# Experts' products on fp32 operands in place of three products of split parts, in a gated attention and mixture-of-experts block

## The chip, the cores and the metric

The kernel runs on one NeuronCore of a Trainium2 chip. The metric is the device time of one execution in microseconds (us), as the median of three executions. TensorE multiplies; VectorE, ScalarE and GpSimd work beside it, and SyncE issues most DMAs.

## The reference, cut to what matters

The block takes 4096 tokens (32 sequences of 128) of width 256. First comes cross attention with 16 heads of 64, which ends in a residual sum. Then comes a mixture of 8 experts, to which the change belongs: every token is sent to its two best experts, each expert takes at most 1024 tokens, and the experts' outputs are weighted and added to the residual.

```
logits = xf @ gate_w.T;  scores = softmax(logits);  topv, topi = top_k(scores, 2)
gates = topv / sum(topv);  flat_idx = topi * cap + loc          # cap = 1024
disp[flat_idx] += xf * valid;  de = disp.reshape(8, 1024, 256)
h  = relu(einsum("ecd,ehd->ech", de, fc1_w) + fc1_b)            # 1024 hidden
eo = einsum("ech,ehd->ecd", h, fc2_w) + fc2_b
x  = x + tanh(g_ffn) * sum(gathered(eo) * gates)
```

All arrays are fp32.

## The kernel before, in words

The program has two parts in one block, each written out in full by Python loops, with one instruction stream per engine and semaphores between them.

`attention` handles 8 groups of 4 sequences. It projects queries, keys and values, forms scores, exponentials, transposes and weighted values, projects out, adds the residual, and routes the tokens. GpSimd then scatters each token's normalised row into the table `disp` in device memory with 8 indirect DMAs for a group (`dispatch`, line 395). The last group's tail is `finish`, and each engine has one.

`experts` handles 8 experts of 1024 token slots each, in two halves of 512: 16 groups, numbered n = 2e + half. For a group, TensorE does the following in this order (line 1136 on):

- the upward products: 8 blocks m of 128 hidden units, each contracting two parts k of 128 features over 512 tokens, into one of two PSUM banks `up`;
- 8 transposes of the next group's rows into `rT` (line 1133);
- the downward products: for 4 blocks i of 128 tokens, 8 parts k of the hidden units, 256 output columns, into `down[i]`. Blocks 0 and 1 run interleaved, then block 2, then block 3.

Most of the kernel's large products don't take fp32 operands. An fp32 tensor is written as a high part (a copy to the type fp32r, on ScalarE: `high`, `split_high`, `high_rows`) and a low part (the tensor minus its high part, also fp32r: `low` and `low_rows` on VectorE, `split_low` on GpSimd). A product is then three: high by high, high by low, low by high (lines 1149 to 1151 and 1163 to 1165). Six fp32 uses remain: transposes, scores (L533), weighted values (L521), the routing logits (L565 and L648), the two rank products (L571 and L572), and the 16 filler products on the identity at the start (L109), which keep TensorE occupied while loads run.

For each expert SyncE loads `fc1` and `fc2` (1 MB each) into `w1_raw` and `w2_raw`. ScalarE and GpSimd split them into one of two pairs of split buffers. For expert 0 the split is made inside the attention's `finish`: two ScalarE copies (lines 740 and 748) and two VectorE subtractions (lines 962 and 986), which signal `s_e0_lo`. The hidden activations go from PSUM to `hid` by ScalarE with bias and relu (line 1199), then VectorE makes `hid_h` and `hid_l` (lines 1250 and 1252). After the downward products VectorE adds the bias (line 1259), ScalarE scales by the gate (line 1207) and GpSimd adds the rows into the output with 4 indirect DMAs for a group (line 1095).

Between the two parts TensorE runs fillers: 40 products on `wk_h` at the end of attention and 6 on `w1_h` ahead of the first expert group (line 1173).

Of the kernel before, what the change touches and what calls it, by code (L numbers as in the profile page):

```python
# [5 lines left out]
P = 128  # L6
# [64 lines left out]
def gated_block(nc, x, ctxT, g_x, g_f, wq, wk, wv, wo, bo, gateT, fc1T, fc1b, fc2, fc2b, out):  # L71
# [6 lines left out]
    with ExitStack() as keep:  # L78
# [17 lines left out]
        s_e0_lo = sem("e0_lo")  # L96
        shared = (s_e0_lo, first, blank, running, tanh_g, ident, w1_raw, w2_raw, w1_split, w2_split)
# [19 lines left out]
def attention(nc, ctx, block, sem, x_v, out_v, disp, ctxT, g_x, g_f, wq, wk, wv, wo, bo, gateT, fc1T, fc2, shared):  # L117
# [7 lines left out]
    s_e0_lo, first, blank, running, tanh_g, ident, w1_raw, w2_raw, w1_split, w2_split = shared  # L125
# [48 lines left out]
    def ps(name):  # L174
# [14 lines left out]
        s_dve_self, s_pool_self, s_dve_gate, s_pool_gate, s_e0_in, s_c0_hi, s_e0_hi,  # L189
# [8 lines left out]
        "dve_self", "pool_self", "dve_gate", "pool_gate", "e0_in", "c0_hi", "e0_hi",  # L198
# [239 lines left out]
    def _(pe):  # L438
# [185 lines left out]
        def wait_warm(count):  # L624
            keep_warm(nc, key_bank, wk_h[:, 0:P], wk_h[:, 0:TOK], count)
# [33 lines left out]
    def _(act):  # L659
# [73 lines left out]
        def finish():  # L733
# [5 lines left out]
            act.wait_ge(s_e0_in, 32)  # L739
            high(wq_h[:, :, :], w1_raw[:, :, :]).then_inc(s_e0_hi, 1)  # L740
# [6 lines left out]
            act.wait_ge(s_o_ready, 2 * NG)  # L747
            high(wo_h[:, :, :], w2_raw[:, :, :]).then_inc(s_e0_hi, 1)
# [6 lines left out]
    def _(dve):  # L755
# [195 lines left out]
        def finish():  # L951
# [9 lines left out]
            dve.wait_ge(s_e0_hi, 1)  # L961
            low(wq_l[:, :, :], w1_raw[:, :, :], wq_h[:, :, :]).then_inc(s_e0_lo, 1)
# [31 lines left out]
def experts(nc, ctx, block, sem, out_rows, disp, fc1T, fc1b, fc2, fc2b, shared):  # L994

    f32, f32r, i32, u32 = mybir.dt.float32, mybir.dt.float32r, mybir.dt.int32, mybir.dt.uint32
    ALU, ACT, AX = mybir.AluOpType, mybir.ActivationFunctionType, mybir.AxisListType.X
# [5 lines left out]
    s_e0_lo, first, blank, running, tanh_g, ident, w1_raw, w2_raw, w1_split, w2_split = shared  # L1003
    w1_h, w1_l = [w1_split[0], sb("w1_h1", [P, DK, H], f32r)], [w1_split[1], sb("w1_l1", [P, DK, H], f32r)]
    w2_h, w2_l = [w2_split[0], sb("w2_h1", [P, HK, D], f32r)], [w2_split[1], sb("w2_l1", [P, HK, D], f32r)]
    eo = [sb(f"eo_{n}", [P, GB, D]) for n in range(2)]
    rT_h, rT_l = sb("rT_h", [P, DK, TOK], f32r), sb("rT_l", [P, DK, TOK], f32r)
    hid = [sb(f"hid{n}", [P, TOK]) for n in range(2)]
    sb("line_up_hid", [P, LINE_UP])
    hid_h, hid_l = sb("hid_h", [P, HK, TOK], f32r), sb("hid_l", [P, HK, TOK], f32r)  # L1010
# [8 lines left out]
    def ps(name):  # L1019
# [7 lines left out]
        s_w_in, s_w_hi, s_w_lo, s_b_in0, s_b_in1, s_rows0, s_rows1,  # L1027
        s_rt_ready, s_rt_hi, s_rt_split, s_up_ready, s_hid, s_hid_hi, s_hid_split, s_down_ready, s_eo_raw,
        s_eo_raw2, s_eo_ready, s_scatter0, s_scatter1, s_meta, s_dve_self, s_pool_gate,
    ) = (sem("e_" + name) for name in (  # L1030
        "w_in", "w_hi", "w_lo", "b_in0", "b_in1", "rows0", "rows1",
        "rt_ready", "rt_hi", "rt_split", "up_ready", "hid", "hid_hi", "hid_split", "down_ready", "eo_raw",
# [4 lines left out]
    biases = [s_b_in0, s_b_in1]  # L1037

    disp_v = disp.rearrange("(e s) w -> e s w", e=E)
    EB = 2  # L1040
    TURNS = E // EB

    @block.sync
    def _(sp):
# [4 lines left out]
        def step(e, nxt, par, first=False):  # L1049

            if first:
                sp.wait_ge(s_e0_lo, 2)
            else:
                sp.wait_ge(s_w_lo, e)
            load_expert(sp, fc1T, fc2, nxt, w1_raw, w2_raw, s_w_in)
            if not first:
                sp.wait_ge(s_eo_raw2, 2 * e)
            load_bias(nxt, 1 - par)
            for half in range(2):
                n = 2 * e + half  # L1060
                sp.wait_ge(s_meta, n + 1)
                load_rows(nxt, half)
# [8 lines left out]
        step(0, 1, 0, True)  # L1071
        step(1, 2, 1)
        for t in range(1, TURNS - 1):
            for i in range(EB):
                step(EB * t + i, EB * t + i + 1, i)
        step(E - 2, E - 1, 0)
        step(E - 1, E - 1, 1)
        sp.wait_ge(s_w_in, 32 * E)
        sp.wait_ge(biases[0], 32 * (E // 2 + 1))
        sp.wait_ge(biases[1], 32 * (E // 2))  # L1080
        for half in range(2):
            sp.wait_ge(rows_in[half], 16 * (E + 1))
            sp.wait_ge(scatters[half], 16 * GB * E)

    @block.gpsimd
    def _(pool):
        def scatter(n, e, par, half):
            if half == 0 and not (isinstance(e, int) and e == 0):
                for done in scatters:
                    pool.wait_ge(done, 16 * GB * e)  # L1090
# [10 lines left out]
        def split_low(e, par):  # L1101

            pool.wait_ge(s_w_hi, 2 * e - 1)
            for k in range(DK):
                nc.gpsimd.tensor_tensor(w1_l[par][:, k, :], w1_raw[:, k, :], w1_h[par][:, k, :].bitcast(f32), ALU.subtract)
            pool.wait_ge(s_w_hi, 2 * e)
            nc.gpsimd.tensor_tensor(w2_l[par][:, :, :], w2_raw[:, :, :], w2_h[par][:, :, :].bitcast(f32),
                                    ALU.subtract).then_inc(s_w_lo, 1)

        def step(e, par):  # L1110

            split_low(e + 1, 1 - par)
            for half in range(2):
                scatter(2 * e + half, e, par, half)

        step(0, 0)
        step(1, 1)
        for t in range(1, TURNS):
            for i in range(EB):
                step(EB * t + i, i)  # L1120
# [4 lines left out]
    def _(pe):  # L1125
        mm = nc.tensor.matmul

        def transpose_rows(loads, half):

            pe.wait_ge(rows_in[half], loads)  # L1130
# [5 lines left out]
        def group(n, e, par, half):  # L1136

            for m in range(HK):
                if not (isinstance(n, int) and n == 0 and m < 2):
                    pe.wait_ge(s_hid, 8 * n + m - 1)  # L1140
                if m == 0:
                    pe.wait_ge(s_rt_split, 2 * n + 2)
                    if isinstance(e, int) and e == 0:
                        pe.wait_ge(s_e0_lo, 2)
                    else:
                        pe.wait_ge(s_w_lo, e)
# [7 lines left out]
            transpose_rows(16 * (e + 1) if half == 0 else 16 * (e + 2), 1 - half)  # L1154

            for k, i in [(k, i) for tiles in ((0, 1), (2,), (3,)) for k in range(HK) for i in tiles]:
                if i == 0:
                    pe.wait_ge(s_hid_split, 8 * n + k + 1)
                if k == 0 and not (isinstance(n, int) and n == 0):
                    pe.wait_ge(s_eo_raw, 4 * n - 3 + i)  # L1160
                t = slice(i * P, (i + 1) * P)
                o = down[i][:, 0:D]
# [136 lines left out]
```

## Time and profile before

| | us |
|---|---|
| time, median of 3 runs | 1035.96 (1035.08 to 1039.14) |
| profiled execution, its own time | 1036.79 |
| profiled execution, its span | 1034.9 |
| TensorE busy | 962.2 (93%) |
| VectorE busy | 642.1 (62%) |
| ScalarE busy | 504.6 (49%) |
| GpSimd busy | 359.9 (35%) |
| TensorE's share of the chain that ended last | 70% |

The profile is one execution. The span runs from the first to the last recorded instruction. L12 means line 12 of the kernel; PE is TensorE, PEld its weight loads, DVE VectorE, ACT ScalarE, POOL GpSimd and SP SyncE. A matmul's shown duration reaches from its start to its last result, and consecutive matmuls overlap, so the pace of a stream is the distance from one start to the next, not the duration. Where a view merges k equal instructions into one row, its duration is k - 1 such distances plus the duration of one.

### The profile page before, as it was taken

The numbers are of one execution on the slowest core, as the hardware profiler recorded it, in microseconds if no ns is written. First come the engines' busy times: TensorE is split into PE (matmuls) and PEld (weight loads), VectorE is DVE, ScalarE is ACT, GpSimd is POOL, SyncE is SP. The second block draws the span as 40 slices with busy tenths as digits, with TensorE's granted clock in tenths as the row PEclk, the third lists the DMA queues.
The fourth block names the chain that finished last, engine by engine and source line by source line (L and its number), as shares of the span: only waits on it lengthen the run. The fifth ranks groups of instructions, "written<-read, shape, count | busy, mean of one in ns | idle before, by whom it ended". The sixth has DMA issues, their size and how long they took to land.

```text
span 1034.9 us, 18912 instructions
## 1 busy us (share of the span) xinstructions
PE 962.2 (93%) x7158; PEld 838.1 (81%) x7158; DVE 642.1 (62%) x1517; ACT 504.6 (49%) x1564; POOL 359.9 (35%) x319
## 2 busy tenths in 40 slices
PE   7799998998998998999989977699999999999996
PEld 5587887887877877878868865599999999999995
DVE  5677586685785785875865764455555555554553
ACT  3576465564563663663763631345353535434352
POOL 6711025024033042051031053064554626355553
PEclk8999999999999999999998998899999999999999
DMA  8195002011020020020110011542426244242522
GB/s 249 44 284 165 22 30 75 22 58 45 22 78 28 21 88 16 22 78 6 42 42 23 20 40 44 163 122 47 127 42 161 76 101 123 47 119 42 134 61 31
DMA packets 63097, 76.60 MB, mean 74 GB/s; under 512 B 6033, under 2 KB 55096, under 8 KB 63008
## 3 DMA queue, kind: packets, MB, share of 16 engines
q1 hardware_dynamic: 50720, 59.18, 18.8%
q0 software_dynamic: 12288, 16.23, 7.9%
q8 instruction: 57, 0.93, 0.4%
q14 instruction: 32, 0.26, 0.1%
HBM read 46.52 MB, written 29.49 MB: 73 GB/s over the span
## 4 chain that ended last, share of the span: by engine, by line
PE 70%; ACT 10%; DVE 8%; POOL 4%; issue 3%; DMA 2%; another core or an unknown queue 2%; SPq 1%; POOLq 0%; DVEq 0%
PE down L1164 6%; PE down L1163 6%; PE down L1165 6%; PE up L1149 6%; PE up L1150 6%; PE up L1151 6%; PE out_bank L521 4%; PE probT L508 4%; PE score L533 4%; ACT probs_odd L690 3%; ACT work L690 3%; PE rT L1133 2%; PE query_bank L454 2%; PE query_bank L452 2%
## 5 line engine op out<-in xcount | busy, mean ns | idle before, releaser
L1095 POOL DMA_INDIRECT out_dram<-eo,index x64 | 105.1, 1642 | 98.3 <-ACT eo L1207 70.2
L1199 ACT ACTIVATE hid<-up,b 128x512 f32<-128x512 f32 x128 | 88.3, 690 | 84.4 <-PE up L1151 79.7
L690 ACT ACTIVATE work<-score,negmax 128x128 f32<-128x128 f32 x256 | 91.0, 380 | 48.8 <-DVE negmax L869 43.5
L690 ACT ACTIVATE probs_odd<-score,negmax 128x128 f32<-128x128 f32 x256 | 91.1, 382 | 47.7 <-DVE negmax L869 47.7
L395 POOL DMA_INDIRECT disp<-packed,slots x64 | 65.0, 1015 | 126.9 <-DVE slots L860 109.8
L1259 DVE TENSOR_TENSOR eo_raw<-down,b 128x256 f32<-128x256 f32 x64 | 26.0, 424 | 123.3 <-PE down L1165 123.3
L877 DVE COPY pT<-probT 128x512 f32<-128x512 f32 x128 | 82.3, 682 | 31.8 <-remote 21.8
L661 ACT ACTIVATE k_sb<-key_bank 128x512 f32<-128x512 f32 x64 | 39.0, 609 | 127.7 <-PE key_bank L477 127.7
L869 DVE TENSOR_REDUCE negmax<-score 128x4 f32<-128x512 f32 x128 | 82.2, 680 | 23.8 <-PE score L533 13.7
L533 PE MATMUL score<-k_sb,q_sb 64*128 64x128 f32 x1024 | 72.3, 282 | 26.1 <-ACT q_sb L661 25.6
L533 PEld LDWEIGHTS score<-k_sb,q_sb 64*128 64x128 f32 x1024 | 68.0, 193 | 33.2 <-ACT q_sb L661 30.6
L1252 DVE TENSOR_TENSOR hid_l<-hid,hid_h 128x512 fp32r<-128x512 f32 x128 | 88.6, 692 | 4.4
L1207 ACT ACTIVATE eo<-eo_raw,gate 128x256 f32<-128x256 f32 x64 | 30.9, 506 | 120.8 <-DVE eo_raw L1259 120.8
L521 PE MATMUL out_bank<-pT,v_sb 128*64 128x128 f32 x1008 | 75.8, 297 | 3.7 <-DVE aT_l L761 1.9
L1250 DVE CAST hid_h<-hid 128x512 fp32r<-128x512 f32 x128 | 55.3, 432 | 32.5 <-ACT hid L1199 31.5
L1163 PE MATMUL down<-w_split,hid_h 128*128 128x256 f32 x256 | 72.0, 281 | 0.0
L1163 PE MATMUL down<-w_h,hid_h 128*128 128x256 f32 x256 | 72.0, 281 | 0.0
L1164 PE MATMUL down<-w_split,hid_h 128*128 128x256 f32 x256 | 71.3, 279 | 0.0
L1165 PE MATMUL down<-w_split,hid_l 128*128 128x256 f32 x256 | 71.3, 279 | 0.0
L1164 PE MATMUL down<-w_l,hid_h 128*128 128x256 f32 x256 | 71.3, 279 | 0.0
L1165 PE MATMUL down<-w_h,hid_l 128*128 128x256 f32 x256 | 71.3, 279 | 0.0
L521 PEld LDWEIGHTS out_bank<-pT,v_sb 128*64 128x64 f32 x1008 | 59.3, 147 | 12.4 <-DVE xT_l L761 3.1
(231 smaller groups left out, 2835.5 us busy)
## 6 DMA issues: line engine op xcount, KB each, us to landing
rows<-disp SPq DMA_DIRECT2D x18, 516.0 KB, 5.7
w_raw<-fc1T_dram SPq DMA_DIRECT2D x9, 1024.0 KB, 7.0
w_raw<-fc_dram SPq DMA_DIRECT2D x9, 1024.0 KB, 11.5
disp<-fixed SPq DMA_DIRECT2D x1, 8256.0 KB, 34.1
rows<-x_dram SPq DMA_DIRECT2D x16, 512.0 KB, 4.2
out_dram<-rows SPq DMA_DIRECT2D x8, 512.0 KB, 2.9
c_raw<-ctxT_dram SPq DMA_DIRECT2D x8, 256.0 KB
c_raw<-ctxT_dram SPq DMA_DIRECT2D x16, 128.0 KB
```

The lines of the kernel that those rows point to most:

```text
L395: pool.indirect_dma_start(out=disp[:, :], out_offset=bass.IndirectOffsetOnAxis(ap=slots[:, j, b:b + 1], axis=0), in_=packed[:, b, :], in_o ...
L521: last = mm(bank[hh * DH:(hh + 1) * DH, b * P:(b + 1) * P], v_sb[:, j // 4, b, cols], pT[:, hh, b * P:(b + 1) * P], start=True, stop=True)
L533: last = mm(score[hh][:, t], q_sb[r, t], k_sb[u % 2][r, t], start=True, stop=True)
L690: last = nc.scalar.activation(probs[w % 2][:, c, :], score[hh][:, b * P:(b + 1) * P], ACT.Exp, bias=negmax[:, w % 2, c:c + 1], accum_out=s ...
L869: V.tensor_reduce(negmax[:, w % 2, hh * GB:(hh + 1) * GB], score[hh][:, :].rearrange("p (i k) -> p i k", i=GB), axis=AX, op=ALU.max, negat ...
L877: V.tensor_copy(pT[:, hh, :], probT[hh][:, :]).then_inc(pt_done, 1)
L1095: pool.indirect_dma_start(out=out_rows[:, :], out_offset=bass.IndirectOffsetOnAxis(ap=index[half][:, i:i + 1], axis=0), in_=eo[half][:, i, ...
L1163: mm(o, hid_h[:, k, t], w2_h[par][:, k, :], start=(k == 0), stop=False)
L1164: mm(o, hid_h[:, k, t], w2_l[par][:, k, :], start=False, stop=False)
L1165: last = mm(o, hid_l[:, k, t], w2_h[par][:, k, :], start=False, stop=(k == HK - 1))
L1199: nc.scalar.activation(hid[m % 2][:, :], up[m % 2][:, :], ACT.Relu, bias=b1[par][:, m:m + 1]).then_inc(s_hid, 1)
L1252: V.tensor_tensor(hid_l[:, m, :], hid[m % 2][:, :], hid_h[:, m, :].bitcast(f32), ALU.subtract).then_inc(s_hid_split, 1)
```

## The change

The experts take `w1`, `w2`, the rows and the hidden activations as fp32. Each product of three becomes one. The weights of odd experts are loaded into a second fp32 pair, `w1_odd` and `w2_odd`, those of even experts into `w1_raw` and `w2_raw`. All splits of the experts' operands go, those of expert 0 in the attention's `finish` too. The first half of the transposed rows is copied out of PSUM by ScalarE and the second by VectorE. The load of an expert's weights waits for the downward products of the expert that used the buffer. The loads, biases and transposes that the old loops issued past the last expert are gone, and so are the 6 fillers; the 40 fillers read `wq_h`. A new semaphore `s_att_out` tells SyncE that the attention's memory is free for the first load into the second pair.

```diff
@@ attention, scalar, finish
-            act.wait_ge(s_e0_in, 32)
-            high(wq_h[:, :, :], w1_raw[:, :, :]).then_inc(s_e0_hi, 1)
...
-            act.wait_ge(s_o_ready, 2 * NG)
-            high(wo_h[:, :, :], w2_raw[:, :, :]).then_inc(s_e0_hi, 1)
@@ attention, vector, finish
-            dve.wait_ge(s_e0_hi, 1)
-            low(wq_l[:, :, :], w1_raw[:, :, :], wq_h[:, :, :]).then_inc(s_e0_lo, 1)
...
-            dve.wait_ge(s_e0_hi, 2)
-            low(wo_l[:, :, :], w2_raw[:, :, :], wo_h[:, :, :]).then_inc(s_e0_lo, 1)
             dve.wait_ge(s_first_done, 1)
+            dve.wait_ge(s_o_done, 2 * NG)
+            dve.sem_inc(s_att_out, 1)
@@ experts, buffers
+    w1 = [w1_raw, sb("w1_odd", [P, DK, H])]
+    w2 = [w2_raw, sb("w2_odd", [P, HK, D])]
+    rT_sb = sb("rT_sb", [P, DK, TOK])
+    hid = sb("hid", [P, HK, TOK])
@@ experts, sync
+        def step(e):
+            nxt, par = e + 1, (e + 1) % 2
+            if nxt < E:
+                if e == 0:
+                    sp.wait_ge(s_att_out, 1)
+                else:
+                    sp.wait_ge(s_down_ready, 8 * e)
+                load_expert(sp, fc1T, fc2, nxt, w1[par], w2[par], weights[par])
+                if e > 0:
+                    sp.wait_ge(s_eo_raw2, 2 * e)
+                load_bias(nxt, par)
+                for half in range(2):
+                    n = 2 * e + half
+                    sp.wait_ge(s_meta, n + 1)
+                    sp.wait_ge(s_rt_ready, 2 * n + 2)
+                    load_rows(nxt, half)
@@ experts, tensor, upward
-                    mm(up[m % 2][:, :], w1_h[par][:, k, c], rT_h[:, k, :], start=(k == 0), stop=False)
-                    mm(up[m % 2][:, :], w1_h[par][:, k, c], rT_l[:, k, :], start=False, stop=False)
-                    last = mm(up[m % 2][:, :], w1_l[par][:, k, c], rT_h[:, k, :], start=False, stop=(k == DK - 1))
+                    last = mm(up[m % 2][:, :], w1[par][:, k, c], rT_sb[:, k, :], start=(k == 0), stop=(k == DK - 1))
@@ experts, tensor, downward
-                mm(o, hid_h[:, k, t], w2_h[par][:, k, :], start=(k == 0), stop=False)
-                mm(o, hid_h[:, k, t], w2_l[par][:, k, :], start=False, stop=False)
-                last = mm(o, hid_l[:, k, t], w2_h[par][:, k, :], start=False, stop=(k == HK - 1))
+                last = mm(down[i][:, 0:D], hid[:, k, i * P:(i + 1) * P], w2[par][:, k, :], start=(k == 0), stop=(k == HK - 1))
@@ experts, scalar
+        def rows_out(n):
+            act.wait_ge(s_rt_ready, 2 * n + 1)
+            nc.scalar.activation(rT_sb[:, 0, :], rT[0][:, :], ACT.Copy).then_inc(s_rt0_done, 1)
...
-                nc.scalar.activation(hid[m % 2][:, :], up[m % 2][:, :], ACT.Relu, bias=b1[par][:, m:m + 1]).then_inc(s_hid, 1)
+                nc.scalar.activation(hid[:, m, :], up[m % 2][:, :], ACT.Relu, bias=b1[par][:, m:m + 1]).then_inc(s_hid, 1)
@@ experts, vector
-            for m in range(HK):
-                dve.wait_ge(s_hid, 8 * n + m + 1)
-                V.tensor_copy(hid_h[:, m, :], hid[m % 2][:, :]).then_inc(s_hid_hi, 1)
-                dve.wait_ge(s_hid_hi, 8 * n + m + 1)
-                V.tensor_tensor(hid_l[:, m, :], hid[m % 2][:, :], hid_h[:, m, :].bitcast(f32),
-                                ALU.subtract).then_inc(s_hid_split, 1)
+        def rows_out(n):
+            dve.wait_ge(s_rt_ready, 2 * n + 2)
+            V.tensor_copy(rT_sb[:, 1, :], rT[1][:, :]).then_inc(s_rt1_done, 1)
```

## Rows read from the trace of the kernel before

**Rows 1.** Busy time in stretches: us from:to, its length, then each engine busy (instructions):
```profile
692.44:715.53 23.09, 23.09 (x154) 21.15 (x152) 12.55 (x27) 8.45 (x14) 6.18 (x4) 1.00 0.44 86
738.62:761.30 22.68, 22.68 (x153) 20.74 (x152) 12.47 (x27) 8.42 (x14) 6.18 (x4) 1.00 0.42 84
```

**Rows 2.** Timeline of TensorE in one group: start us, us, instruction:
```profile
800.27 0.39 PE L1149 MATMUL up<-rT_h,w_h 128*128 128x512 f32 x1
...
806.85 0.39 PE L1151 MATMUL up<-rT_h,w_l 128*128 128x512 f32 x1
807.08 1.03 PE L1133 MATMUL rT<-ident,rows 128*128 128x128 f32 x8
808.07 0.28 PE L1164 MATMUL down<-w_l,hid_h 128*128 128x256 f32 x1
...
819.14 0.28 PE L1165 MATMUL down<-w_h,hid_l 128*128 128x256 f32 x1
```

**Rows 3.** Timeline of TensorE, its fp32 products in attention:
```profile
3.66 1.70 PE L109 MATMUL key_bank<-ident 128*128 128x128 f32 x7
7.81 0.83 PE L109 MATMUL key_bank<-ident 128*128 128x128 f32 x6
134.44 1.84 PE L565 MATMUL query_bank<-gate_sb,work 128*128 128x8 f32 x16
```

**Rows 4.** Single lines: count, duration ns min/median/max, first and last start:
```profile
L109 PE MATMUL key_bank<-ident x32: 274/275/579, 3.3 to 8.4; 128*128 128x128 f32 x32
L1149 PE MATMUL up<-rT_h,w_h x128: 389/389/396, 704.6 to 1012.6; 128*128 128x512 f32 x128
L1164 PE MATMUL down<-w_l,hid_h x256: 276/281/283, 716.5 to 1024.8; 128*128 128x256 f32 x128
L565 PE MATMUL query_bank<-gate_sb,work x112: 170/256/257, 134.4 to 586.2; 128*128 128x8 f32 x112
```

**Rows 5.** Timelines of ScalarE and GpSimd behind the last product:
```profile
1025.69 0.51 ACT L1207 ACTIVATE eo<-eo_raw,gate 128x256 f32<-128x256 f32 x1 [2.21 <-DVE eo_raw L1259]
1027.59 1.55 POOL L1095 DMA_INDIRECT out_dram<-eo,index  x1 [0.30 <-issue]
```

**Rows 6.** The attention's tail: one line's durations, then timelines of three engines:
```profile
L378 POOL TENSOR_TENSOR rows<-rows,bias_o x32: 717/728/2877, 92.2 to 618.9; 128x256 f32<-128x256 f32 x32
602.80 1.11 POOL L395 DMA_INDIRECT disp<-packed,slots  x1 [34.10 <-DVE slots L860]
615.32 2.29 DVE L761 TENSOR_TENSOR w_split<-w_raw,w_split 128x2048 fp32r<-128x2048 f32 x1 [1.11 <-ACT w_split L661]
622.77 0.28 PE L548 MATMUL value_bank<-w_split,aT_l 128*128 128x256 f32 x1
623.47 0.74 DVE L895 SCALAR_TENSOR_TENSOR rows<-value_bank,fixed,rows 128x512 f32<-128x512 f32 x1
637.20 2.29 DVE L761 TENSOR_TENSOR w_split<-w_raw,w_split 128x2048 fp32r<-128x2048 f32 x1
638.01 2.45 POOL L395 DMA_INDIRECT disp<-packed,slots  x1 [10.80 <-DVE slots L860]
```

**Rows 7.** Before group 0: clock (third from last), then timelines of TensorE and VectorE:
```profile
648.22:658.46 10.24, 3.67 (x13) 3.28 (x14) 1.38 (x2) 1.19 (x2) 0.97 (x1) 0.50 0.62 159
654.79 1.97 PE L1133 MATMUL rT<-ident,rows 128*128 128x128 f32 x8 [9.68 <-DMA rows<-disp]
657.43 0.69 DVE L1242 TENSOR_TENSOR rT_l<-rT,rT_h 128x512 fp32r<-128x512 f32 x1 [0.16 <-ACT rT_h L1190]
658.82 0.40 PE L1149 MATMUL up<-rT_h,w_split 128*128 128x512 f32 x1
```

**Rows 8.** Costliest groups (busy, mean ns | idle before), waits, DMA issues (landing):
```profile
L1199 ACT ACTIVATE hid<-up,b 128x512 f32<-128x512 f32 x128 | 88.3, 690 | 84.4 <-PE up L1151 79.7
PE rT L1133 <- DMA rows<-disp: 9.7, 1, 9.7
w_raw<-fc_dram SPq DMA_DIRECT2D x9, 1024.0 KB, 11.5
```

More of the change, by code:

```diff
@@ L1070, in _ @@
         load_bias(0, 0)
[L1071 to L1080, printed above, removed]
+        for e in range(E):
+            step(e)
         for half in range(2):
-            sp.wait_ge(rows_in[half], 16 * (E + 1))
             sp.wait_ge(scatters[half], 16 * GB * E)
@@ L1086, in _, with scatter @@
     def _(pool):
-        def scatter(n, e, par, half):
-            if half == 0 and not (isinstance(e, int) and e == 0):
+        def scatter(n, e, half):
+            if half == 0 and e > 0:
                 for done in scatters:
@@ L1099, in scatter @@
                     compute_op=ALU.add).then_inc(scatters[half], 16)
[L1101 to L1120, printed above, removed]
+        for n in range(2 * E):
+            scatter(n, n // 2, n % 2)
         for done in scatters:
@@ L1126, in _, with transpose_rows @@
         mm = nc.tensor.matmul
-        def transpose_rows(loads, half):
-            pe.wait_ge(rows_in[half], loads)
+        def transpose_rows(n):
+            e, half = divmod(n, 2)
+            pe.wait_ge(rows_in[half], 16 * (e + 1))
+            if n > 0:
+                pe.wait_ge(s_rt0_done, n)
+                pe.wait_ge(s_rt1_done, n)
             for k in range(DK):
@@ L1134, in transpose_rows, with group @@
                 last.then_inc(s_rt_ready, 1)
-        def group(n, e, par, half):
+        def group(n, e):
+            par = e % 2
             for m in range(HK):
-                if not (isinstance(n, int) and n == 0 and m < 2):
+                if n > 0 or m > 1:
                     pe.wait_ge(s_hid, 8 * n + m - 1)
                 if m == 0:
-                    pe.wait_ge(s_rt_split, 2 * n + 2)
-                    if isinstance(e, int) and e == 0:
-                        pe.wait_ge(s_e0_lo, 2)
+                    pe.wait_ge(s_rt0_done, n + 1)
+                    pe.wait_ge(s_rt1_done, n + 1)
+                    if e == 0:
+                        pe.wait_ge(s_e0_in, 32)
@@ L1152, in group @@
                 last.then_inc(s_up_ready, 1)
-            transpose_rows(16 * (e + 1) if half == 0 else 16 * (e + 2), 1 - half)
+            if n + 1 < 2 * E:
+                transpose_rows(n + 1)
             for k, i in [(k, i) for tiles in ((0, 1), (2,), (3,)) for k in range(HK) for i in tiles]:
                 if i == 0:
-                    pe.wait_ge(s_hid_split, 8 * n + k + 1)
-                if k == 0 and not (isinstance(n, int) and n == 0):
+                    pe.wait_ge(s_hid, 8 * n + k + 1)
+                if k == 0 and n > 0:
@@ L1166, in group @@
                 if k == HK - 1:
                     last.then_inc(s_down_ready, 1)
-        def wait_warm(count):
-            keep_warm(nc, down[0], w1_h[0][:, 0, 0:P], w1_h[0][:, 0, 0:TOK], count)
-        transpose_rows(16, 0)
-        wait_warm(6)
-        for n in range(2 * EB):
-            group(n, n // 2, n // 2, n % 2)
-        for t in range(1, TURNS):
-            for i in range(2 * EB):
-                group(2 * EB * t + i, EB * t + i // 2, i // 2, i % 2)
+        transpose_rows(0)
@@ L1180, in _ @@
+        for n in range(2 * E):
+            group(n, n // 2)
     @block.scalar
     def _(act):
-        def split_high(e, par):
-            act.wait_ge(s_w_in, 32 * e)
-            nc.scalar.activation(w1_h[par][:, :, :], w1_raw[:, :, :], ACT.Copy).then_inc(s_w_hi, 1)
-            nc.scalar.activation(w2_h[par][:, :, :], w2_raw[:, :, :], ACT.Copy).then_inc(s_w_hi, 1)
-        def high_rows(n):
-            for k in range(DK):
-                act.wait_ge(s_rt_ready, 2 * n + k + 1)
-                nc.scalar.activation(rT_h[:, k, :], rT[k][:, :], ACT.Copy).then_inc(s_rt_hi, 1)
@@ L1208, in group @@
                                      scale=gate[half][:, i:i + 1]).then_inc(s_eo_ready, 1)
-        high_rows(0)
-        for n in range(2 * EB):
-            group(n, n // 2, n // 2, n % 2)
-        for t in range(1, TURNS):
-            for i in range(2 * EB):
-                group(2 * EB * t + i, EB * t + i // 2, i // 2, i % 2)
+        rows_out(0)
+        for n in range(2 * E):
+            group(n, n // 2, n % 2)
     @block.vector
@@ L1223, in meta @@
             dve.wait_ge(rows_in[half], 16 * (e + 1))
-            if not (isinstance(e, int) and e == 0):
+            if e > 0:
                 dve.wait_ge(scatters[half], 16 * GB * e)
@@ L1261, in group @@
             dve.sem_inc(s_eo_raw2, 1)
-        low_rows(0)
-        for n in range(2 * EB):
-            group(n, n // 2, n // 2, n % 2)
-        for t in range(1, TURNS):
-            for i in range(2 * EB):
-                group(2 * EB * t + i, EB * t + i // 2, i // 2, i % 2)
+        rows_out(0)
+        for n in range(2 * E):
+            group(n, n // 2, n % 2)
 def kernel(**inputs):
```

81 lines of the change are left out of this document (28 added, 53 removed).

## The prediction

> **What bounds the kernel now.** I read the table of stretches first, because the change touches only what comes after 613 us and nearly all of it after 655. In an expert group all 23.09 or 22.68 us are TensorE's [rows 1]; VectorE has work for 12.5 us of it, ScalarE for 8.4 and GpSimd for 6.2. The list of waits for this part names TensorE once, 9.7 us for the very first rows, while ScalarE stands 79.7 us waiting for TensorE's upward products [rows 8]. So the experts' time is the number of TensorE's instructions times their pace, and the splits that the change removes lie wholly beside it. What they cost VectorE, ScalarE and GpSimd buys nothing. The question is only whether one fp32 product takes less time on TensorE than three fp32r products.
>
> The 16 groups run from 658.82 [rows 7] to the end of the last product (its last instructions start from 1024.8 on, at 0.118 us each, and end at about 1025.2 [rows 4]): 366.4 us, 22.9 a group.
>
> **The products before.** From the timeline of one group [rows 2]: upward, 30 products start between 800.27 and 806.85, 6.58/29 = 0.227 us from start to start for 512 columns. Downward, from 808.07 to 819.14 lie 94 distances, 11.07/94 = 0.118 us for 256 columns. That group is one of the slower kind; the groups alternate between 23.09 and 22.68 us [rows 1], and if I put this difference on the 96 downward products the other pace is 0.1135 and the mean 0.1156. A group has 8 x 2 x 3 = 48 upward and 4 x 8 x 3 = 96 downward products: 48 x 0.227 + 96 x 0.1156 = 10.9 + 11.1 = 22.0 us; the rest is 8 transposes, 7 x 0.108 and a start.
>
> **The products after.** There will be 16 upward and 32 downward products in a group. The trace has no fp32 product of 256 or 512 columns, so the price comes from narrower ones. First, each fp32 product is recorded as two matmul instructions: the 16 fillers on the identity stand as 32 [rows 4]. Second, such an instruction of 128 columns follows its forerunner after (1.70 - 0.42)/6 = 0.213 us early and after (0.83 - 0.275)/5 = 0.111 us a little later [rows 3], the first at the lower level of TensorE's clock and the second at the upper (one is 256 cycles of 1.2 GHz, the other 267 of 2.4). So the instruction costs two cycles a column, the product four, where three fp32r products cost three plus some stalls (0.227 us is 545 cycles for 512 columns). The durations agree: fp32r goes from 281 ns at 256 columns to 389 at 512, 108 ns for 256 more, which leaves 173 ns at no columns; the fp32 instruction of 128 columns takes 275, and its 102 ns above 173 are two cycles a column again [rows 4].
>
> For a wide fp32 instruction the choice is in the stalls:
>
> - none: 0.4267 us upward and 0.2133 downward; a group 32 x 0.4267 + 64 x 0.2133 = 27.3 us of products;
> - a fixed 5 ns an instruction, as the row with 128 columns has over its 256 cycles: 0.4316 and 0.2182, so 13.8 + 14.0 = 27.8 us;
> - in proportion, each pass as dear as an fp32r pass: 0.454 and 0.231, so 14.5 + 14.8 = 29.3 us.
>
> I take the second, since it is read from an fp32 row; at 128 columns the proportional cost would be 0.113, above the 0.111 of the row. Per group 27.8 - 22.0 = +5.8 us, for 16 groups +92.8 (ends: +85 and +117). The last group's transposes of rows that nobody used go: 8 x 0.108 = -0.9. Together **+91.9 us**.
>
> The Trainium skill says in FP8 and Floating Point Precision (TensorE Precision Notes) that a true fp32 product is four passes through the array and that fp32r reads four bytes and truncates. By that rule four passes stand in place of three, 4/3 of 22.0 us, an estimate of +117 us over the 16 groups; the rows above show the same two passes an instruction but a lower stall.
>
> **What could wait now and doesn't.** Upward, TensorE needs a `up` bank back after two blocks; ScalarE's relu takes 0.69 us [rows 8] and a block now lasts 4 x 0.43 = 1.7 us where it lasted 1.36, so that wait gets looser. Downward products wait for `hid` itself, without VectorE's two steps between. The rows' copies have a whole stretch of downward products (14 us) to hide in. Weights for expert e + 1 are issued when expert e begins and have about 57 us for a landing of 11.5 [rows 8]; the rows, issued behind them on SyncE's queue with waits for the bias buffer, the gates and the transposes, are needed at the earliest 14 us after the group they are issued in has begun, and for the first half it is one group (28 us) later. GpSimd has 4 indirect DMAs of 1.55 us in 28 us [rows 5]. All of these I cost at nothing.
>
> **The attention's tail.** GpSimd's bias sum L378 takes 0.7 to 1.2 us but once 2.88, and the first dispatch DMA of the last group 2.45 against 1.11 in the group before; both coincide with one of the two 2.29 us VectorE subtractions that go [rows 6]. The first gives up to 1.7 us on the first half of the last group, but the second half is bound by the product that ends at 622.9, so only about 0.4 passes on to the residual at 623.47. The second gives 2.45 - 1.11 = 1.3. The rows for group 0 then land at about 653.0 in place of 654.8.
>
> **The first group.** Before, the 6 fillers hold TensorE until 658.82, though the operands are ready at 657.43 + 0.69 = 658.1 [rows 7]. After, transposes take 653.0 to 655.0, ScalarE and VectorE copy side by side (under 0.7 us each, as the row of VectorE's subtraction), and the upward products start at about 655.8. The clock was at half level from 648.22 to 658.46 [rows 7]. If it comes back at the same moment, 2.7 us at half pace do 1.3 us of work, and the gain over before is 658.8 - 655.8 - 1.3 = 1.7 us. If it comes back some 3 us later nothing is left. I take -1.2, ends -1.7 and +2.
>
> **The tail.** Before, the last indirect DMA starts at 1027.59, 0.30 us after the one ahead of it has left the engine, although its operand is ready at 1025.69 + 0.51 = 1026.2 [rows 5]. Now block 3 takes 16 x 0.218 = 3.5 us, more than GpSimd's 1.55 + 0.30 us a DMA, so the queue is empty when it comes. I take -0.6, ends -1.2 and 0.
>
> **Sum.** 1034.9 + 91.9 - 1.2 - 0.6 = 1125.0 us of span. The profiled execution took 1.9 us more than its span, so 1126.9, and the median of the runs is 0.8 below that execution: **1126 us**.
>
> **Rivals.**
>
> 1. *The fp32 row is bound by loading weights, not by columns* (the other side). An fp32 product of only 8 columns has the same pace: 16 instructions in 1.84 us, about 0.11 each [rows 3]. Then nothing on pace forces the second cycle a column, and an fp32 instruction of 512 columns might cost one pass, 0.227. A group would be 32 x 0.227 + 64 x 0.1156 = 14.7 us of products, -7.3, and the kernel 1036 - 117 - 3 = about 916 us. It decides if the pass count is under three a product. Against it: the durations, 170 ns at the least for 8 columns and 275 for 128, whose difference is two cycles a column [rows 4]; but the ends of matmuls are modelled. The skill's rule above speaks against it too. Chance 0.04.
> 2. *Each pass stalls like an fp32r pass.* +117 instead of +92.8: about 1150 us. For it: fp32r's 6% over its cycles at both widths. Against it: the fp32 row. Chance 0.24.
> 3. *A stall that the slower pace uncovers or the clock doesn't stay up.* A clock that fell to half in the fp32 stream would double 27.8 us a group, to some 1570 us; the rows with fp32 products alone saw it rise [rows 3]. A small version, a few us per expert for late rows or weights, gives 1140 to 1170. Chance 0.05 together.
> 4. *The gain elsewhere pays for it.* That would need 90 us out of waits that the list does not show [rows 8]. Chance 0.01, which I count as no change.
>
> My forecast has 0.66. Its own range is 1117 (no stalls, both ends of head and tail at their best) to 1134. The range that holds 8 in 10 reaches up to the proportional case: 1114 to 1153. Within 0.5% of 1036 is what a measurement can't tell from no change; faster by more 0.04, same 0.01, slower 0.95.
>
> **What would show it.** Right: two matmul instructions a product, paces near 0.432 and 0.218 us, groups of 28.7 us, TensorE still full in them, VectorE's share there down to a few us, the first dispatch DMA of the last group at 1.1 us, first upward product at about 656. Wrong: upward pace near 0.227 (rival 1) or 0.454 (rival 2), gaps between TensorE's instructions, or a half-level clock inside the groups.

## The result, and the profile after

| | before | after |
|---|---|---|
| median time, us (4 runs each) | 1035.52 (1034.03 to 1039.14) | 1123.32 (1121.99 to 1124.62) |
| profiled execution, its own time, us | 1036.79 | 1124.40 |
| its span, us | 1034.9 | 1122.6 |

The changed kernel takes 1.084 times as long (95% interval 1.081 to 1.086), 88 us more. The forecast was 1126 with a range of 1114 to 1153.

The first lines of the page: engine busy time, share of the span, instructions.

```profile
span 1122.6 us, 16931 instructions
PE 1050.5 (94%) x6376; PEld 808.4 (72%) x6376; DVE 484.0 (43%) x1241; ACT 463.4 (41%) x1528; POOL 275.9 (25%) x295
```

Three engines lost a great deal of work (VectorE 158 us, ScalarE 41, GpSimd 84) and TensorE lost 782 matmul instructions. It is busy for 88 us more all the same. Fewer instructions, more time: those of the experts' products got longer. One middle group and its place in the table of stretches (columns as in [rows 1]):

```profile
715.98 13.90 PE L1122 MATMUL up<-rT_sb,w_odd 128*128 128x512 f32 x32
729.71 1.04 PE L1104 MATMUL rT<-ident,rows 128*128 128x128 f32 x8
730.58 13.98 PE L1133 MATMUL down<-w_odd,hid 128*128 128x256 f32 x64
744.40 1.02 PE L1122 MATMUL up<-rT_sb,w_odd 128*128 128x512 f32 x2
```

```profile
715.98:744.40 28.42, 28.42 (x106) 19.07 (x105) 3.10 (x10) 7.91 (x13) 6.15 (x5) 1.00 0.45 116
656.92:1113.10 456.18, 456.18 (x1656) 304.90 (x1656) 48.44 (x158) 125.55 (x206) 96.67 (x63) 1.00 0.30 68
656.92:661.00 4.08, 4.08 (x5) 1.80 (x6) 0.71 (x5) 0.24 (x1) 0.00 (x0) 0.50 1.01 359
661.00:1113.10 452.10, 452.10 (x1652) 303.10 (x1650) 47.73 (x153) 125.31 (x206) 96.67 (x63) 1.00 0.30 65
```

A group takes 28.42 us where it took 22.68 or 23.09 [rows 1], and TensorE has not a moment free in it. For the pace I need the duration of one instruction:

```profile
L1122 PE MATMUL up<-rT_sb,w_odd x256: 592/592/593, 716.0 to 1098.8; 128*128 128x512 f32 x128
L1133 PE MATMUL down<-w_odd,hid x512: 379/379/382, 730.6 to 1112.8; 128*128 128x256 f32 x171
```

Upward (13.90 - 0.592)/31 = 0.4293 us, downward (13.98 - 0.379)/63 = 0.2159 us. Two cycles a column at 2.4 GHz are 0.4267 and 0.2133; what is above them is 2.6 ns in both. Each group's 16 upward products stand as 32 instructions, two a product, as the fillers of [rows 4] do.

The places at the edges: GpSimd at the first DMA of the last group's dispatch and TensorE at the first group (against [rows 6, 7]), and GpSimd at the end (against [rows 5]):

```profile
638.70 1.10 POOL L395 DMA_INDIRECT disp<-packed,slots  x1 [11.05 <-DVE slots L856]
...
654.12 1.97 PE L1104 MATMUL rT<-ident,rows 128*128 128x128 f32 x8 [8.91 <-DMA rows<-disp]
656.92 9.67 PE L1122 MATMUL up<-rT_sb,w_raw 128*128 128x512 f32 x17 [0.83 <-issue]
...
1112.18 1.54 POOL L1080 DMA_INDIRECT out_dram<-eo,index  x1 [0.30 <-issue]
1115.33 1.54 POOL L1080 DMA_INDIRECT out_dram<-eo,index  x1 [1.61 <-issue]
```

From the start of that dispatch to the first upward product it is now 18.2 us, where it was 20.8. But 17 upward instructions take 9.67 us there: the first ones run at half level (granted clock 0.50 up to 661 us, 1.00 behind it). At the end GpSimd waits 1.61 us for its last operand instead of being late.

The ledger of the 87.7 us of span, profile against profile: up to the start of the last group's dispatch +0.7; dispatch to first product -2.6; the 16 groups +89.9, made of 16 x 5.53 for the pace, 2.2 for the half-level start of group 0 and -0.9 for the last group's 8 transposes; after the last product -0.3.

### The profile page after: what moved, and what is told of

Same layout as the page of the kernel before. It is cut to its first block, busy times and chain, and to the rows that moved or that the text cites. A ratio compares the mean times of both kernels' runs of the same rounds, so it can differ in the third digit from the quotient of the medians.

```text
span 1122.6 us, 16931 instructions
## 1 busy us (share of the span) xinstructions
PE 1050.5 (94%) x6376; PEld 808.4 (72%) x6376; DVE 484.0 (43%) x1241; ACT 463.4 (41%) x1528; POOL 275.9 (25%) x295
## 4 chain that ended last, share of the span: by engine, by line
PE 73%; ACT 9%; DVE 8%; POOL 3%; DMA 2%; issue 2%; another core or an unknown queue 2%; SPq 1%; POOLq 0%; DVEq 0%
PE up L1122 20%; PE down L1133 20%; PE out_bank L521 4%; PE probT L508 3%; PE score L533 3%; ACT probs_odd L690 3%; ACT work L690 3%; DVE negmax L865 2%; PE query_bank L546 1%; PE query_bank L452 1%; PE query_bank L454 1%; PE query_bank L548 1%; PE query_bank L547 1%; PE query_bank L453 1%
## 5 line engine op out<-in xcount | busy, mean ns | idle before, releaser
L1080 POOL DMA_INDIRECT out_dram<-eo,index x64 | 98.8, 1544 | 369.3 <-ACT eo L1161 309.2
L1122 PE MATMUL up<-rT_sb,w_raw 128*128 128x512 f32 x256 | 113.4, 601 | 0.8 <-issue 0.8
L1133 PE MATMUL down<-w_raw,hid 128*128 128x256 f32 x512 | 111.8, 379 | 0.0
L1133 PE MATMUL down<-w_odd,hid 128*128 128x256 f32 x512 | 111.8, 379 | 0.0
L1122 PE MATMUL up<-rT_sb,w_odd 128*128 128x512 f32 x256 | 111.2, 592 | 0.0
L1133 PEld LDWEIGHTS down<-w_odd,hid 128*128 128x128 f32 x512 | 96.7, 190 | 13.3 <-issue 0.5
L1133 PEld LDWEIGHTS down<-w_raw,hid 128*128 128x128 f32 x512 | 96.7, 190 | 12.8
L1192 DVE COPY rT_sb<-rT 128x512 f32<-128x512 f32 x16 | 11.1, 692 | 216.5 <-PE rT L1104 216.5
L533 PE MATMUL score<-k_sb,q_sb 64*128 64x128 f32 x1024 | 73.2, 285 | 30.5 <-ACT q_sb L661 30.1
L533 PEld LDWEIGHTS score<-k_sb,q_sb 64*128 64x128 f32 x1024 | 69.1, 196 | 37.6 <-ACT q_sb L661 34.9
L1122 PEld LDWEIGHTS up<-rT_sb,w_raw 128*128 128x128 f32 x256 | 49.3, 193 | 60.3 <-issue 60.0
L1122 PEld LDWEIGHTS up<-rT_sb,w_odd 128*128 128x128 f32 x256 | 48.6, 190 | 57.8 <-issue 57.4
```

Of the source, the lines that this page charges most:

```text
L533: last = mm(score[hh][:, t], q_sb[r, t], k_sb[u % 2][r, t], start=True, stop=True)
L1080: pool.indirect_dma_start(out=out_rows[:, :], out_offset=bass.IndirectOffsetOnAxis(ap=index[half][:, i:i + 1], axis=0), in_=eo[half][:, i, ...
L1122: last = mm(up[m % 2][:, :], w1[par][:, k, c], rT_sb[:, k, :], start=(k == 0), stop=(k == DK - 1))
L1133: last = mm(down[i][:, 0:D], hid[:, k, i * P:(i + 1) * P], w2[par][:, k, :], start=(k == 0), stop=(k == HK - 1))
```

## The experiments

Two chips served these runs. On the one of e1 to e8 the kernel before took 999.6 us (beside e1 to e4) and 1002.8 (beside e5 to e8), on the one of e9 and e10 1034.2; each kernel is compared with the kernel before on its own chip. Of e4, e7 and e8 there is one execution each (1134.9, 1091.5 and 1119.9 us), and only rows of their traces are read.

**e1 and e2: one kind of product alone.** All of the kernel before stays, its splits, waits and fillers too; only the low parts are left out of the sums.

```diff
 e1, upward
-    mm(up[m % 2][:, :], w1_h[par][:, k, c], rT_h[:, k, :], start=(k == 0), stop=False)
-    mm(up[m % 2][:, :], w1_h[par][:, k, c], rT_l[:, k, :], start=False, stop=False)
-    last = mm(up[m % 2][:, :], w1_l[par][:, k, c], rT_h[:, k, :], start=False, stop=(k == DK - 1))
+    last = mm(up[m % 2][:, :], w1_h[par][:, k, c].bitcast(f32), rT_h[:, k, :].bitcast(f32), start=(k == 0), stop=(k == DK - 1))
 e2, downward
-                mm(o, hid_h[:, k, t], w2_h[par][:, k, :], start=(k == 0), stop=False)
-                mm(o, hid_h[:, k, t], w2_l[par][:, k, :], start=False, stop=False)
-                last = mm(o, hid_l[:, k, t], w2_h[par][:, k, :], start=False, stop=(k == HK - 1))
+    last = mm(o, hid_h[:, k, t].bitcast(f32), w2_h[par][:, k, :].bitcast(f32), start=(k == 0), stop=(k == HK - 1))
```

> The kernel before with all its splits, loads and waits, and only the upward products replaced: one fp32 product of the high parts in place of three fp32r products (the low parts are left out of the sum). Theory A, the price is TensorE's passes: 32 instructions of 0.429 us in place of 48 of 0.227, +2.8 us a group, +45 us in all, about 1081. Theory B, part of the 88 us comes from the new buffers and waits of the change: clearly under +45.

> The kernel before with only the downward products replaced by one fp32 product of the high parts (the low parts are left out of the sum). Theory A: 64 instructions of 0.216 us in place of 96 of 0.1165, +2.6 us a group, +42 us in all, about 1078. Theory B: clearly under +42.

Measured, two runs each: e1 1045.9 us against 999.6, ratio 1.047 (1.038 to 1.055), +46.3. e2 1043.3, ratio 1.044 (1.041 to 1.047), +43.7. Both as theory A has it. In the traces the experts' part, from the first upward product to the start of the last downward one, is 42.6 us longer in e1 and 43.5 in e2 than in the kernel before.

**e3: both kinds.**

> The kernel before with both kinds of products replaced and everything else kept: splits on three engines, fillers, single raw buffers, loads past the end. Theory A: +87 us, about 1123, as slow as the changed kernel, since all else that the change removes lies beside TensorE; the difference to the changed kernel is the tail and the last transposes, 1 to 3 us. Theory B: under +80, the rest comes from the new structure.

Measured, two runs: 1087.7 us against 999.6, ratio 1.088 (1.085 to 1.092), +88.2, the same step as the whole change (+87.8). The expected time was written for a chip on which the kernel before takes 1036; the step is what counts. The steps of e1 and e2 add up to 46.3 + 43.7 = 90.0, which is the same within the runs' spread. From its second group on, each takes 28.42 us, as in the changed kernel. Its engines (the page's first part):

```profile
PE 1037.1 (95%) x6390; PEld 800.2 (74%) x6390; DVE 642.8 (59%) x1517; ACT 504.0 (46%) x1564; POOL 348.9 (32%) x319
```

VectorE, ScalarE and GpSimd do all that they did before, and the kernel is no slower than the one in which they don't.

**e5: the subtractions gone, the three products kept.** Most of the other half of the change alone: VectorE and GpSimd no longer make low parts. ScalarE's copies and VectorE's `hid_h` stay, since the fp32r products read them. The sums count the high parts three times.

```diff
-    mm(up[m % 2][:, :], w1_h[par][:, k, c], rT_l[:, k, :], start=False, stop=False)
-    last = mm(up[m % 2][:, :], w1_l[par][:, k, c], rT_h[:, k, :], start=False, stop=(k == DK - 1))
+    mm(up[m % 2][:, :], w1_h[par][:, k, c], rT_h[:, k, :], start=False, stop=False)
+    last = mm(up[m % 2][:, :], w1_h[par][:, k, c], rT_h[:, k, :], start=False, stop=(k == DK - 1))
...
-    low(wo_l[:, :, :], w2_raw[:, :, :], wo_h[:, :, :]).then_inc(s_e0_lo, 1)
+    dve.sem_inc(s_e0_lo, 1)
```

> The kernel before with all the experts' subtractions gone (VectorE's, GpSimd's, and the two of expert 0), and each product still three fp32r products, now of the high parts alone (so the output lacks the low parts and counts the high one three times). It is the other half of the change alone: the split work without the product. Theory A, the splits lie beside TensorE: 1 to 2 us faster, all of it at the attention's tail, no change within a group. Rival, the splits hold TensorE back somewhere: more than 5 us faster.

Measured: 1002.3 us against 1002.8, ratio 0.9991 (0.9974 to 1.0008): no change that can be measured. The 1 to 2 us at the tail stay within the interval; in its profile the first DMA of the last group's dispatch takes 1.10 us and the first product comes 19.4 us after that DMA's start, where it was 20.8. Two of its groups (columns as in [rows 1]):

```profile
668.80:691.89 23.09, 23.09 (x154) 21.15 (x153) 5.75 (x17) 12.02 (x16) 5.98 (x5) 1.00 0.29 52
691.89:714.57 22.68, 22.68 (x154) 20.74 (x153) 5.74 (x17) 8.42 (x14) 6.07 (x4) 1.00 0.55 140
```

They last as long as before, to 0.01 us [rows 1], with less than half of VectorE's work in them. So the products cost 88 us (e3), and taking the subtractions off two engines returns less than 3 (e5). What ScalarE's copies alone return was not run; e3, which keeps them, costs what the whole change costs.

**e4 and e8: the price by width.** Rows of filler products at the end of the changed kernel's attention, each row on a line of its own: 16 products in e4, mostly 24 in e8. The first two rows of e4 and one of e8:

```diff
             wait_warm(40)
+            pe.wait_ge(s_e0_in, 32)
+            wf, wr = w1_raw[:, 0, :], wq_h[:, 0, :]
+            for n in range(16):
+                mm(key_bank[:, 0:512], wf[:, 0:P], wf[:, 0:512], start=True, stop=True)
+            for n in range(16):
+                mm(key_bank[:, 0:256], wf[:, 0:P], wf[:, 0:256], start=True, stop=True)
...
+            for n in range(24):
+                mm(key_bank[0:64, 0:64], wf[:, 0:64], wf[:, 0:64], start=True, stop=True)
```

> The changed kernel with ten rows of 16 filler products at the end of attention: fp32 with 512, 256, 128, 64 and 8 columns, fp32r with 512, 256, 128 and 64, and fp32 with weights of 64 columns. Theory A (two cycles a column and instruction, a small fixed stall, and a floor from loading weights): fp32 instructions at 0.429, 0.216, 0.111, then 0.11 for 64 and 8 columns. If the 5 ns over 256 cycles at 128 columns were the instruction's own stall, 64 columns would come at 0.06. If it is the weights, 64 columns of weights at 512 moving columns change nothing. fp32r: 0.227, 0.113 to 0.118, and at 128 and 64 columns either half of that again or the weights' floor; if fp32r takes four passes at narrow widths, 0.11 twice or more.

> The changed kernel with rows of 24 filler products at the end of attention: fp32 with weights of 128 columns and 8 moving; fp32 with weights of 64 columns and 128, 64, 8 moving; fp32r with 128 columns of weights and 512, 256 moving; fp32r with 64 columns of weights and 512, 256, 128, 64 moving. Theory A, the 0.1117 us that all narrow products share is the loading of 128 weight columns: with 64 columns it halves to about 0.056 where few columns move, fp32 with 128 moving falls only to 0.109, its own two cycles a column, and fp32r with 256 moving falls from 0.114-0.120 to 0.109. Rival, a fixed cost per instruction: all stay at 0.11.

Timelines of TensorE (stretches at the clock's lower level are left out). The weights (the stationary operand) have 128 or 64 columns: 128*64 means 64. w_raw is fp32, w_split fp32r. First e4, then e8:

```profile
608.44 13.89 PE L656 MATMUL key_bank<-w_raw 128*128 128x512 f32 x32
622.17 7.07 PE L658 MATMUL key_bank<-w_raw 128*128 128x256 f32 x32
629.08 3.73 PE L660 MATMUL key_bank<-w_raw 128*128 128x128 f32 x32
632.65 3.68 PE L662 MATMUL key_bank<-w_raw 128*128 128x64 f32 x32
...
646.68 2.08 PE L668 MATMUL key_bank<-w_split 128*128 128x256 f32 x16
648.59 1.90 PE L670 MATMUL key_bank<-w_split 128*128 128x128 f32 x16
650.33 1.97 PE L672 MATMUL key_bank<-w_split 128*128 128x64 f32 x16
```

```profile
624.73 2.89 PE L660 MATMUL key_bank<-w_raw 128*64 128x128 f32 x25
...
627.57 2.96 PE L662 MATMUL key_bank<-w_raw 128*64 128x64 f32 x48
630.37 2.92 PE L664 MATMUL key_bank<-w_raw 128*64 128x8 f32 x48
638.81 3.03 PE L668 MATMUL key_bank<-w_split 128*128 128x256 f32 x24
...
647.20 2.89 PE L672 MATMUL key_bank<-w_split 128*64 128x256 f32 x24
649.93 1.60 PE L674 MATMUL key_bank<-w_split 128*64 128x128 f32 x24
651.37 1.54 PE L676 MATMUL key_bank<-w_split 128*64 128x64 f32 x24
```

I take off one instruction's duration (592, 379, 275 and 275 ns for the fp32 rows of e4) and divide by the number of distances. fp32 with 512 columns is (13.89 - 0.592)/31 = 0.429 us, 256 columns 0.216, 128 columns 0.111, 64 columns 0.110. From 128 columns down it falls no more. With weights of 64 columns it does: (2.96 - 0.222)/47 = 0.058 for 64 columns and (2.92 - 0.203)/47 = 0.058 for 8. And fp32 with 128 moving columns then takes (2.89 - 0.273)/24 = 0.109, its own two cycles a column and 2.4 ns. So in these rows there is a floor, and it goes with the columns of the weights: 0.111 us for 128, 0.058 for 64. The rival of a fixed cost per instruction falls. A wide product doesn't feel it: fp32 with 512 moving columns and weights of 64 stays at 0.429 us in e4.

The floor is there for fp32r too: about 0.11 us for 128 as for 64 columns, and with weights of 64 columns (1.60 - 0.222)/23 = 0.060 for 128 columns and (1.54 - 0.223)/23 = 0.057 for 64. At 256 columns fp32r lies just above it, (3.03 - 0.283)/23 = 0.119, and with weights of 64 columns (2.89 - 0.276)/23 = 0.114 (0.109 was expected). That this difference comes from the weights is not shown: with weights of 128 columns the kernel before runs its downward products at 0.114 and 0.119 us by turns, and e1 runs the same products at 0.114 in every group. Which of the two paces a group gets, and what is left above 0.107, is open.

**e7: a subtraction put back.** The changed kernel, with the second of VectorE's two removed subtractions at its old place as dead work.

```diff
+            low(wo_l[:, :, :], w2_raw[:, :, :], wo_h[:, :, :])
             dve.wait_ge(s_first_done, 1)
             dve.wait_ge(s_o_done, 2 * NG)
```

> The changed kernel with one of the removed VectorE subtractions (2.29 us, a dead one here) put back at its old place, ahead of the last dispatch. Theory A, it holds GpSimd's descriptor writing back: the first dispatch DMA takes about 2.45 us again in place of 1.10 and the first expert product comes 1.3 us later. Rival, the 2.45 was something else: 1.1 us stays.

Its timelines of VectorE and GpSimd:

```profile
604.18 2.29 DVE L757 TENSOR_TENSOR w_split<-w_raw,w_split 128x2048 fp32r<-128x2048 f32 x1
...
604.99 2.45 POOL L395 DMA_INDIRECT disp<-packed,slots  x1 [11.05 <-DVE slots L856]
607.75 0.97 POOL L395 DMA_INDIRECT disp<-packed,slots  x1 [0.30 <-issue]
```

2.45 us again, and GpSimd's DMA instruction ends 0.97 us after the subtraction does, the length of an undisturbed one: it stands still while this subtraction of two SBUF operands runs. Whether other VectorE work does the same was not run. From that DMA's start to the first product it is 19.5 us, against 18.2: the 1.3 that was expected.

**e6: one fp32r product of the high parts.** As e5, with one product where there were three.

> As the one before, but with one fp32r product of the high parts in place of three. Theory A (TensorE bound until another engine is): TensorE's products of a group fall from 22.0 to 7.4 us, and ScalarE, with 8 relus of 0.6 us, two row copies, half a weight split of 3.8 and four scalings, becomes the bound at 10 to 12 us a group; so 170 to 200 us faster. If instead something beside TensorE paced the groups already, far less.

Measured: 836.6 us against 1002.8, ratio 0.835 (0.832 to 0.838), -166. The low parts of weights, rows and activations are left out of the sums. It is the version with fewer passes, and faster than both kernels; whether an application can spare the low parts is a question of precision that time does not answer. The saving is a little under the 170 to 200 expected, and TensorE is no longer the bound. Three waits of its experts' part: who waited for whom, us in total, times, longest us.

```profile
POOL out_dram L1095 <- ACT eo L1200: 67.8, 14, 9.5
PEld up L1146 <- ACT hid L1192: 63.1, 84, 2.6
PE up L1146 <- ACT hid L1192: 28.2, 28, 2.2
```

TensorE now waits for ScalarE's relu in the upward products. Nor is its clock always at the upper level: the granted clock is 0.90 on average from 623 to 820 us.

**e9: the relus shared out.** ScalarE writes the even blocks as fp32r directly, VectorE the odd ones.

```diff
-            for m in range(HK):
+            for m in range(0, HK, 2):
                 act.wait_ge(s_up_ready, 8 * n + m + 1)
...
-                nc.scalar.activation(hid[m % 2][:, :], up[m % 2][:, :], ACT.Relu, bias=b1[par][:, m:m + 1]).then_inc(s_hid, 1)
+                nc.scalar.activation(hid_h[:, m, :], up[m % 2][:, :], ACT.Relu, bias=b1[par][:, m:m + 1]).then_inc(s_hid, 1)
...
+            for m in range(1, HK, 2):
+                dve.wait_ge(s_up_ready, 8 * n + m + 1)
+                V.tensor_scalar(hid_h[:, m, :], up[1][:, :], b1[par][:, m:m + 1], 0.0, ALU.add, ALU.max).then_inc(s_hid_hi, 1)
+            low_rows(n + 1)
             meta(n, e, half)
-            for m in range(HK):
...
```

The edit does one thing more: in the kernel before and in e6 VectorE makes a group's gates (`meta`) ahead of its work on the hidden blocks, in e9 behind it.

> One fp32r product of the high parts as in e6, and the hidden activations written as fp32r at once, even blocks by ScalarE and odd ones by VectorE, so that no copy stands between. Theory A, e6's groups are paced by the loop of upward product, relu and copy over two banks: that loop gets shorter, a group falls from 11.3 to 9 us, 30 to 40 us under e6, ratio 0.79 to 0.81 of the kernel before. Rival, the indirect DMAs or the loads pace the groups already: within 10 us of e6.

Measured: 869.5 us against 1034.2, ratio 0.839 (0.837 to 0.841), -165: what e6 saved, no more. Nothing of the 30 to 40 us came; from the first upward product to the start of the last downward one it is 202.0 us, against 196.6 in e6. A stretch of the experts' part (granted clock, DMA share and GB/s stand last):

```profile
715.00:740.00 25.00, 20.63 (x112) 15.55 (x112) 10.32 (x26) 13.97 (x23) 12.34 (x8) 0.86 0.70 165
```

The clock spends part of the time at half level (0.86 on average), and no engine is full. But this does not refute the theory that the loop paced e6, since the gates moved too. Pieces of the chain of work that ended last, from e6 and then from e9 (start us, us, what):

```profile
712.53 6.97 DMA out_dram<-eo,index
719.70 0.17 DVE index L1222
720.25 0.22 DVE gate L1229
720.48 0.35 DVE hid_h L1243
720.96 0.70 ACT hid L1192
```

```profile
751.45 0.23 DVE gate L1227
751.70 0.38 SPq L1066
752.67 10.01 DMA w_raw<-fc_dram
764.52 1.89 ACT w_h L1178
```

In e6 the gates wait for an earlier group's rows to land in the output, and the copy of the hidden block behind them waits too. In e9 that wait is gone, and another has come: SyncE issues the next rows (L1066) once the gates are there, 142.4 us of waiting from 690 to 860 us, and the expert's weights only behind them, so ScalarE's copies and then TensorE wait for a load of 10 us. That load is 32% of the chain from 665 to 855 us. So what paces an expert in e6, the loop, the landing or the clock, stays open; neither an earlier load nor double buffering was tried here.

**e10: what the edges give, without the products.** The kernel before with its two subtractions behind the last dispatch and 76 fillers in place of 40.

```diff
-            dve.wait_ge(s_e0_hi, 1)
-            low(wq_l[:, :, :], w1_raw[:, :, :], wq_h[:, :, :]).then_inc(s_e0_lo, 1)
...
             dve.wait_ge(s_e0_hi, 2)
+            dve.wait_ge(s_disp, 16 * 2 * GB * NG)
+            low(wq_l[:, :, :], w1_raw[:, :, :], wq_h[:, :, :]).then_inc(s_e0_lo, 1)
             low(wo_l[:, :, :], w2_raw[:, :, :], wo_h[:, :, :]).then_inc(s_e0_lo, 1)
...
-            wait_warm(40)
+            wait_warm(76)
```

> The kernel before with its three products, the two VectorE subtractions of expert 0 moved behind the last dispatch, and 76 fillers in place of 40 to reach up to the rows' arrival. It takes the only gains that the change had beside its products. Theory A: the first dispatch DMA 1.1 us in place of 2.45, and the first group at the upper clock from its first transpose; 2 to 4 us faster, 0.3%. Rival, worth nothing measurable: the fillers run past the rows' arrival and give it back.

Measured: 1032.3 us against 1034.2, ratio 0.9976 (0.9963 to 0.9988), 2 to 2.5 us less. Its GpSimd and TensorE:

```profile
636.87 1.10 POOL L395 DMA_INDIRECT disp<-packed,slots  x1 [10.60 <-DVE slots L860]
...
652.35 1.05 PE L1133 MATMUL rT<-ident,rows 128*128 128x128 f32 x8
653.15 1.63 PE L109 MATMUL down<-w_split 128*128 128x512 f32 x6
654.97 0.50 PE L1149 MATMUL up<-rT_h,w_split 128*128 128x512 f32 x1 [0.19 <-DVE rT_l L1242]
```

From the DMA's start to the first product it is 18.1 us, 2.7 less than before, and the transposes take 1.05 us in place of 1.97, at a granted clock of 1.00 (0.50 before [rows 7]). The shorter DMA is a gain that the change had too. The clock is one that it did not have: its own transposes took 1.97 us.

## Why the prediction was right

*The bound.* TensorE's instructions times their pace, nothing else in the groups. e3 and e5 show it from both sides: all the split work kept, +88; all the subtractions gone, nothing.

*The products before.* 22.0 us a group; from the group of [rows 2] and its faster fellows it is 22.1.

*The products after.* Two instructions a product and two cycles a column were right. The size of the stall was off: I took 5 ns from the row with 128 columns, and the wide instructions have 2.6. e4 and e8 say why: at 128 columns the instruction is not bound by its moving columns at all but by the floor of 0.111 us that goes with 128 columns of weights, so its 5 ns over 256 cycles were no stall of the product. Over 512 upward instructions (0.0024 us each) and 1024 downward ones (0.0023) that is 3.6 us. The measured groups grew by 28.42 - 22.89 = 5.53 us each, +88.5 in all, where the forecast had +92.8; the other 0.7 lies in the 22.1 in place of 22.0, in rounding, and in the steps from one stream to the next.

*Rival 1*, the other side, had half of the truth: the narrow fp32 rows are bound by the weights. Its conclusion, that wide products need only one pass an instruction, is refuted by 0.429 us for 512 columns. The evidence that decided rightly was the durations [rows 4], not the pace of the narrow row.

*Rival 2*, a stall in proportion (0.454 and 0.231 us), is refuted by the same rows. The Trainium skill's rule (FP8 and Floating Point Precision, TensorE Precision Notes: four passes for a true fp32 product) agrees in the pass count here, 2 x 0.429 us for 512 columns. The 4/3 over three fp32r products that the prediction worked out from it, +117 us, does not come out, because an fp32r pass of 0.227 us here costs more than a quarter of the fp32 product, 0.215.

*Rivals 3 and 4* did not come. The clock stayed at the upper level in all groups from 661 us on (granted 1.00), and TensorE had no gap in them.

*Two readings of the prediction.* It took the clock's level in the first filler row [rows 3] from the pace; the profile grants 1.00 there (3.66 to 5.36 us), so its rows alone don't show a lower level. The pace by level, with the granted clock beside it, stands in the change's first group: 5 upward instructions in 4.08 us at 0.50, 0.429 us each at 1.00. And the upper end of the forecast's own range, 1134, does not follow from the ends it names, which give 1130; the time is inside both.

*The attention's tail.* The dispatch DMA fell from 2.45 to 1.10 us as forecast, and e7 shows the cause. The 0.4 us of the other subtraction came too: the last residual starts 0.04 us behind the last product's end, where it was 0.42. *The first group.* First product at 656.92, not 655.8: that last product itself ended 0.8 us later in this execution and the routing behind it took 0.3 longer, for reasons that I don't know, so the dispatch started 0.7 us later and not 0.4 earlier. From transposes to product it took 2.8 us, as forecast. The half-level stretch went on to about 661, later than the better case: of the -1.2 us forecast nothing is left (-2.6, +2.2, and +0.7 ahead of it). *The end.* -0.3, forecast -0.6: GpSimd does wait for its last operand, but takes about 1.15 us from it to the DMA's start.

So against the forecast for the profiled execution, 1126.9, the measured 1124.4 is -4.3 in the groups, +1.5 ahead of them and +0.3 behind them. The mechanism was right, and the size of the stall was the largest error; the smaller errors took back some of it.

## What to carry to other kernels

Where TensorE is full, a product form is priced by passes and columns: the fp32 product cost 4 x 0.215 us for 512 columns here, three fp32r products 3 x 0.227, and what the fp32 form saved on other engines returned nothing, since these had slack. Price a wide product by a wide row; a narrow one may stand at the floor set by its weights. When a heavy engine is the bound, the lever is fewer passes (e6, -166 us, at the price of the low parts), and then look again, since the next bound may be close.

## What was not expected

The floor by weights: in the rows of e4 and e8 with 128 columns of weights products, fp32 or fp32r, settled at about 0.11 us an instruction however few columns moved, with 64 columns at 0.058. An fp32r product with 256 moving columns, 0.114 or 0.119 us, lies hardly above what its weights alone would take. The floor is measured for weights on all 128 partitions. The attention's scores (L533), with weights of 128 columns on 64 partitions, run faster: 16 instructions in 1.05 us, about 0.05 each.

And the two chips. The same attention code runs faster on one of them. Here is the kernel before at 100 to 300 us on the chip where it takes 1035 us, and e1, which has the same attention, on the other:

```profile
100.00:300.00 200.00, 191.68 (x1576) 164.05 (x1574) 142.17 (x359) 108.85 (x435) 45.66 (x55) 0.98 0.11 35
```

```profile
100.00:300.00 200.00, 197.23 (x1677) 168.98 (x1676) 151.75 (x384) 117.67 (x467) 51.66 (x61) 1.00 0.14 47
```

TensorE gets 101 more instructions done in these 200 us on the second, at a granted clock of 1.00 against 0.98. A group of attention takes 69.5 us there against 75.0. The experts' groups are the same on both: 22.68 and 23.09 us in the kernel before and in e5, 28.42 in the changed kernel and in e3. So the step of +88 us is the same too. What makes the difference is open.
